# A state-space block: six other first products for GpSimd, and the last state's product with C for VectorE

## The reference, cut to what matters

```
dA = exp(dt_t[:, :, None] * A)
h  = dA * h + (dt_t * x_t)[:, :, None] * B_t[:, None, :]
y  = einsum('bds,bs->bd', h, C_t)
...
y  = y + xc * D_param
y  = y * silu(z)
```

## Time and profile before

| | |
|---|---|
| median of 3 runs | 16611.66 (16605.69 to 16624.14) |
| the profiled execution: time, span | 16605.28, 16603.5 |
| busy: PE, DVE, ACT, POOL | 14390.7 (87%), 15104.1 (91%), 11266.2 (68%), 15002.7 (90%) |
| granted TensorE clock | 0.941 of full |
| DMA | 152 GB/s of HBM traffic over the span |

### The profile page before, as it was taken

The page is one execution under the profiler, slowest core; times in us unless marked ns, Lnnn a source line. Parts: engine busy times, 40 slices in busy tenths (PEclk is TensorE's granted clock), DMA queues, the critical chain, the costliest instruction groups (busy, mean ns, idle before and its releaser), DMA issues. The chain is left out here.

```text
span 16603.5 us, 158027 instructions
## 1 busy us (share of the span) xinstructions
PE 14390.7 (87%) x30720; PEld 5782.7 (35%) x30720; DVE 15104.1 (91%) x13023; ACT 11266.2 (68%) x18635; POOL 15002.7 (90%) x6275
## 2 busy tenths in 40 slices
PE   6888888888888888888888888888888888888888
PEld 2333333333333333333333333333333333333333
DVE  6999999999999999999999999999999999998988
ACT  5666667666666666666677666667666676667675
POOL 5999889998899989998899998999989999899998
PEclk9999999999999999999999999999999999999999
DMA  3444444444444444444444444444444444444443
GB/s 132 155 154 161 150 152 154 155 157 150 154 154 153 163 145 153 156 154 159 142 155 160 152 160 143 156 156 158 155 143 156 156 157 158 146 148 158 150 151 135
DMA packets 738975, 2535.44 MB, mean 153 GB/s; under 512 B 77240, under 2 KB 78016, under 8 KB 721728
## 3 DMA queue, kind: packets, MB, share of 16 engines
q1 hardware_dynamic: 738112, 2527.45, 44.8%
HBM read 2376.15 MB, written 150.99 MB: 152 GB/s over the span
## 5 line engine op out<-in xcount | busy, mean ns | idle before, releaser
L1467 POOL TENSOR_TENSOR RING<-RING,CS 128x1024 f32<-128x1024 f32 x4096 | 9833.9, 2416 | 1369.6 <-DVE RING L1148 1350.2
L1148 DVE TENSOR_TENSOR_SCAN RING<-DA,HS,RING 128x512 f32<-128x512 f32 x8192 | 9955.4, 1264 | 811.0 <-ACT DA L777 614.1
L388 PE MATMUL YP<-RING,EYE 128*128 128x512 f32 x16384 | 8293.4, 638 | 1648.6 <-POOL RING L1467 1578.7
L777 ACT ACTIVATE DA<-ITEM,AN 128x512 f32<-128x512 f32 x8192 | 5519.4, 685 | 3384.9 <-DVE RING L1148 3376.5
L388 PEld LDWEIGHTS YP<-RING,EYE 128*128 128x128 f32 x16384 | 3133.4, 199 | 6324.9 <-issue 3616.5
L1128 DVE TENSOR_TENSOR RING<-DTP,BS 128x1024 f32<-128x1024 f32 x2816 | 3375.5, 1206 | 0.4 <-DMA BS<-bc_rows 0.3
L1454 POOL TENSOR_TENSOR RING<-ITEM,BS 128x1024 f32<-128x1024 f32 x1280 | 3016.6, 2357 | 9.4
L388 PE MATMUL FL<-XN,WC 128*128 128x512 f32 x4096 | 1943.3, 618 | 9.7 <-ACT XN L864 4.6
L388 PEld LDWEIGHTS FL<-XN,WC 128*128 128x128 f32 x4096 | 839.4, 205 | 1129.8 <-issue 1121.5
L791 ACT ACTIVATE ITEM<-FL,COL 128x512 f32<-128x512 f32 x512 | 347.6, 679 | 1183.1 <-PE FL L388 1183.1
L388 PE MATMUL FL<-LS,WP 128*128 128x512 f32 x2048 | 995.6, 610 | 35.3 <-DVE XR L1184 29.2
(11 more groups left out here) (123 smaller groups left out, 10636.4 us busy)
## 6 DMA issues: line engine op xcount, KB each, us to landing
BS<-bc_rows SPq DMA_DIRECT2D x2048, 512.0 KB, 4.9
CS<-bc_rows SPq DMA_DIRECT2D x2048, 512.0 KB, 3.6
XR<-in_x SPq DMA_DIRECT2D x128, 1024.0 KB, 7.3
x_slices<-XR SPq DMA_DIRECT2D x64, 1024.0 KB, 8.1
XR<-x_slices SPq DMA_DIRECT2D x64, 1024.0 KB, 7.5
out<-XR SPq DMA_DIRECT2D x64, 1024.0 KB, 8.2
XR<-in_wqkv SPq DMA_DIRECT2D x24, 1024.0 KB, 7.3
bc_rows<-ROWS SPq DMA_DIRECT2D x256, 64.0 KB, 4.6
```

Of the source, the lines that this page charges most:

```text
L388: return pe.matmul(*a, **k)
L777: act.activation(DA[:, h, :], DT[:, i % 2, h, :], ACT.Exp, scale=AN[:, h, s:s + 1]).then_inc(dA_ready, 1)
L1148: dve.tensor_tensor_scan(H[:, slot(n), h, :], DA[:, h, :], U[:, slot(n), h, :], HS[:, i % ITEMS, h, s:s + 1], ALU.mult, ALU.add).then_inc( ...
L1467: pool.tensor_tensor(G[:, slot(n)], H[:, slot(n)], CS[:, s % C_ROWS, :].unsqueeze(1).broadcast_to([P, NH, T]), ALU.mult).then_inc(g_ready, 1)
```

## The change

VectorE makes the second product of state 15 right behind its own scan 15 (`out_last`), with a semaphore of its own, `g_last`. GpSimd makes only the second products of states 0 to 14. GpSimd's first products are now those of states 1, 3, 5, 7, 8 and 9, six instead of five; VectorE makes ten instead of eleven, and where it makes them is set anew. The waits on `g_ready` are recounted for 15 products a window, and those on the sixteenth go to `g_last`. In SP's queue the second load of C of a window waits for `g_last`, and the first load of B in a window waits for the second product of state 14 of the window before.

```
-POOL_U = (0, 1, 2, 7, 8)
+POOL_U = (1, 3, 5, 7, 8, 9)
-AHEAD = ((), (), (3,), (4, 5), (6,), (), (), (9,), (10,), (11,), (12,), (13,), (14,), (15,), (), ())
-AHEAD_LATE = ((), (), (3,), (4,), (5, 6), (), (), (9,), (10,), (11,), (12,), (13,), (14,), (15,), (), ())
+AHEAD = ((0,), (), (2,), (4,), (6,), (), (), (), (), (10,), (11, 12,), (13,), (14,), (15,), (), ())
+AHEAD_LATE = ((0,), (), (2,), (4,), (), (6,), (), (), (), (10,), (11,), (12, 13,), (14,), (15,), (), ())
...
+        def pool_g(n):
+
+            return n // NS * (NS - 1) + min(n % NS + 1, NS - 1)
...
                 if not (first and q < 2):
-                    sp.wait_ge(g_ready, tile * STEPS + (n - 2))
+                    if q == 1:
+                        sp.wait_ge(g_last, tile * ITEMS + i)
+                    else:
+                        sp.wait_ge(g_ready, tile * (STEPS - ITEMS) + pool_g(n - 3))
...
                     load_c(tile, w, q, first=first)
+                    if q == 0 and not (first and w == 0):
+                        sp.wait_ge(g_ready, tile * (STEPS - ITEMS) + pool_g(w * NS - 2))
...
-                pe.wait_ge(g_ready, tile * STEPS + n + 1)
+                if s == NS - 1:
+                    pe.wait_ge(g_last, tile * ITEMS + i + 1)
+                else:
+                    pe.wait_ge(g_ready, tile * (STEPS - ITEMS) + pool_g(n))
...
                     dve.wait_ge(state_kept, tile * STEPS + (n - used(n) + 1))
-                    dve.wait_ge(g_ready, tile * STEPS + (n - used(n) + 1))
+                    if (n - used(n)) % NS == NS - 1:
+                        dve.wait_ge(g_last, tile * ITEMS + (n - used(n)) // NS + 1)
+                    else:
+                        dve.wait_ge(g_ready, tile * (STEPS - ITEMS) + pool_g(n - used(n)))
...
+            def out_last(tile, i):
+                n = i * NS + NS - 1
+                q = NS // 2 - 1
+                dve.wait_ge(c_landed[q % (C_ROWS // 2)],
+                            tile * rows_count(ITEMS - 1, NS // 2 - 1, C_ROWS // 2) + rows_count(i, q, C_ROWS // 2))
+                dve.wait_ge(g_summed, tile * STEPS + (n - used(n) + 1))
+                dve.wait_ge(scanned, tile * (2 * STEPS) + 2 * (n + 1))
+                dve.tensor_tensor(G[:, slot(n)], H[:, slot(n)],
+                                  CS[:, (NS - 1) % C_ROWS, :].unsqueeze(1).broadcast_to([P, NH, T]),
+                                  ALU.mult).then_inc(g_last, 1)
...
                     scan(tile, n, first=first)
+                    if s == NS - 1:
+                        out_last(tile, w)
...
-                    out_state(tile, n, first=first)
+                    if s < NS - 1:
+                        out_state(tile, n, first=first)
```

More of the change, by code:

```diff
@@ L142, in block_ssm_kernel @@
             sem(n) for n in ("wc_ready", "wp_folded", "dd_ready", "logsmall_ready", "an_exp", "an_ready", "pbf_ps", "pbf_ready", "mean_ready"))
-        u_dve, u_pool, dA_ready, scanned, g_ready, state_kept, g_summed = (
-            sem(n) for n in ("u_dve", "u_pool", "dA_ready", "scanned", "g_ready", "state_kept", "g_summed"))
+        u_dve, u_pool, dA_ready, scanned, g_ready, g_last, state_kept, g_summed = (
+            sem(n) for n in ("u_dve", "u_pool", "dA_ready", "scanned", "g_ready", "g_last", "state_kept", "g_summed"))
         rows_ready, rows_stored, capped = (sem(n) for n in ("rows_ready", "rows_stored", "capped"))
```

## The result

The changed kernel takes 16916.22 us (median, 16906.51 to 16919.33), the kernel before 16616.29 beside it. The ratio is 1.0179, with a 95% interval of 1.0163 to 1.0195: slower by 300 us. The prediction was 16290 and faster; its range ended at 16640. The profiled execution has a span of 16912.4 us, 308.9 more than before.

What follows compares the result with a forecast made beforehand. VectorE and GpSimd, both 92% busy, were taken to bound the kernel by turns. Window changes of +0.1, -2.5, -1.0 and -1.6 us gave -5.0 a tile, -320 over 64 tiles: 16290 us, range 16000 to 16640.

Steps and rivals of the forecast that it cites:

- the flat price of a contention: VectorE's two-SBUF product of state 15 waits for the running GpSimd instruction: 1.2 to 3.5 us, taken as 2.2.
- 2.0 us a window for both hold-ups: On GpSimd, time lost a window to `dt_poly` and G15 together, added to 24 instructions of 2.31 us.
- rival 2: G15 on VectorE starves through several GpSimd instructions: +920 less the 320, 17200 us; chance 0.05.
- a late `dt_x`: Mid-window GpSimd makes `dt_x` late; ScalarE's copy, the exponential of state 14 and scan 14 wait, replacing the gate's wait.
- net 282 us: Extra VectorE work from gaining G15 and losing a first product: 1.1 us a window, 256 times, if waiting stayed unchanged.
- what can be won is waiting only: Across the engines, no engine has less to do after the change, so any gain must come from waits.
- 320 won in spite of 282 of work: Over the kernel, -5.0 us a tile gives -320 in 64 tiles, although VectorE's added work alone would cost 282.
- the gate is set by G14 and TensorE's order: At the window's end, G14, not G15 alone, sets the gate: 8.9 us from start of sum 14 to end of sum 15.
- the gate's and U2's waits go: At the window's head, the gate's wait nearly goes, from 489 us to under 150, and U2 waits for nobody.
- C and B rows are no cause: In SP's queue, C and B loads wait for G15 and G14 but have slack, about 7 us for B; nothing charged.
- j = 1 was forecast at 62.0: Window j = 1, bound by GpSimd, was to take 61.9 to 62 us against 61.9 before, change +0.1.
- Rival 1: GpSimd's stops move to the window's head, G0, G2, G3 each waiting 1.5 us: +250, 16860 us; chance 0.13.

Runs made afterwards that it cites:

- e9: Changed kernel with GpSimd waiting for `dt_poly` ahead of G10, two instructions earlier, everything computed; 16788.63 us, 128 below the changed kernel.
- e1: Changed kernel with `dt_poly` reading DTP (PSUM) and YZ instead of two SBUF sources, polynomial part of dt left out; 16729.85 us.
- e2: Kernel before with `dt_poly` reading DTP (PSUM) and YZ, polynomial part of dt left out; 16261.55 us, ratio 0.9793 to the kernel before.
- e12: e8 with `dt_poly` reading PSUM, polynomial part of dt left out; 15971.45 us, ratio 0.9612.
- e8: Kernel before with U0 and U2 on VectorE, a step ahead, U3 and U5 on GpSimd, G15 staying there; 16454.01 us, ratio 0.9903.
- e7: Changed kernel with U9 back on VectorE and U9 to U12 at the steps of the kernel before; 16723.36 us, 193 below the changed kernel.
- e13: e7 with both `dt_poly` and the product of state 15 reading PSUM, their true contributions left out; 16255.24 us.
- e14: e8 with GpSimd's wait for `dt_poly` ahead of `dt_first`, one instruction earlier than in e11; 16552.97 us, ratio 0.9971.
- e3: Kernel before with only the product of state 15 moved to VectorE, the plan of first products unchanged; 16865.37 us, ratio 1.0155.
- e4: Kernel before with only the new plan of first products, all 16 second products staying on GpSimd; 16894.96 us, ratio 1.0172.
- e6: Changed kernel with U0 made ahead of scan 15 of the window before and U2 ahead of scan 1; 16891.12 us, 25 below the changed kernel.
- e5: e1 with, besides, the product of state 15 reading DTP (PSUM) in place of H, its true contribution left out; 16373.18 us.
- e11: e8 with GpSimd's wait for `dt_poly` ahead of G10, as in e9, everything computed; 16324.17 us, ratio 0.9820.
- e10: Changed kernel with only the product of state 15 reading DTP (PSUM), its contribution left out; 16777.86 us, 138 below the changed kernel.

## Why the prediction was wrong

**The step that failed first** is the flat price of a contention: "So the product waits for the running GpSimd instruction, then holds the next one up", with `dt_poly` left at its old length and 2.0 us a window for both hold-ups. Only the new product was priced; that the old one, `dt_poly`, could change its price was not asked. Its price is 1.2 us beside an idle GpSimd, some 2.4 with a turn at the first boundary, and 4.6 to 7.6 when it is passed over, since then it waits until GpSimd stops. The change moved three first products into GpSimd's steps 0 to 6, so that in j = 1 `dt_poly` is issued while G9 runs, with `dt_first` and G10 behind it: 7.63 us in place of 2.45, +313 us over the kernel. e9 shows that the stop ends it; e1, e2, e9 and e12 show that the length counts. (Most of the +313 us comes with the first step of the table after e12, where U3 and U5 go to the middle: e8 has 236 of them and is faster all the same.) The earlier trace rows had a maximum of 6241 ns for this line, and rival 2 used the mechanism, but for the product of state 15 alone and "Against: line 1165 takes 2.41". In the sum the contention makes about 200 of the 300 us (543 less 345): by the table after e12 132 in the first step and 75 in the third, less 15 in the second.

On the Trainium skill's page "SBUF — State Buffer", section "Who interferes with whom", the second to issue is blocked until the first finishes. The trace differs: 7.63 us is the rest of one GpSimd instruction and two whole ones that began after VectorE's had been issued. By the page the wait would have ended at 4462.0, with G9; the measurement decides.

**The second failure** is that the wait for the exponential was expected at scan 14, behind a late `dt_x`. It rose by 222 us in all, but at scan 14 it fell from 117 to 80 us, and ScalarE's wait for `dt_x` fell from 244 to 174: `dt_x` was not late. The exponentials are late at steps 4, 5 and 8. Of these e7 and e13 show that step 8 goes with the move of U9 to U12, 193 and 118 us. The rise at steps 4 and 5 is there in e8 too (318 us; 182 before), so it comes with the move of U0, U2, U3 and U5, which e8 shares; what it costs was not tried. The working had followed each engine's count of instructions, but not which of VectorE's products stood beside ScalarE's front work. That a late `dt_x` does cost time is seen only in e14.

**The third failure is the product of state 15.** It was taken at 2.2 us and took 1.72, so its net 282 us were 132; with `dt_poly` gone it takes 3.02 (e1), with the old plan 2.07 (e3). But it was to be paid for by the waits that it ends, and it is not. e3 shows that without the new plan it leaves the gate where it was, e4 that with the new plan the kernel takes as long without it (1.0172 and 1.0179), and e7 beside e8 that it costs 269 us although the gate's wait falls by 165 (240 to 74). Without contention it costs 284. The prediction had said that "what can be won is waiting only". Its own terms, 320 won in spite of 282 of work, need some 600 us less of waiting on VectorE; VectorE's idle time fell by 163 us (1499 to 1337).

**What held:** the gate is set by G14 and TensorE's order (e3, e4); the gate's and U2's waits go, 534 us; C and B rows are no cause (11 us of GpSimd's waits are for C).

**The windows.** j = 1 was forecast at 62.0, j = 2 at 64.9, j = 3 at 62.3, j = 0 at 58.5; in the tile shown they take 65.0, 67.9, 65.4 and 61.1. In the mean over all tiles j = 0 changed by -1.2 (-1.6 was forecast), j = 1 by +2.0 (+0.1), j = 2 by +1.4 (-2.5) and j = 3 by +2.7 (-1.0), so only j = 0 came as forecast. In j = 3 the prediction allowed 0.7 us of waits on VectorE; in the tile shown it idles 5.65 (65.40 less 59.75).

**Rival 1** gave nearly the time (16860), and its sign came true: GpSimd idles as long as before (1341 us for scans, 1350 before). Its mechanism is there in part. The waits of GpSimd's second products at steps 0 to 3 rose from 302 to 613 us, those of G0 alone from 60 to 421, while those at steps 9 and 10 fell from 575 to 274. But in its sum GpSimd's hold-ups are the whole loss, 256 us; measured, GpSimd is busy 150 us more (15153; 15003 before) and idle 159 more. That its time is so close is luck in part. The own-product wait of 0.3 us was not in the sum at all; e6 shows that to remove it gives 25 us.

**What stays open.** What decides whether the waiting instruction has its turn at the first boundary is not settled. In j = 2 of the changed kernel it was passed over 1.2 us after it was issued, in the earlier trace rows it had its turn after 1.3. The 111 us by which e5 is behind e2 are no single cause: by the table after e12 they are -290, +284 and +118. The 118 are shown to go with U9 to U12 together; which of the four moves them, and what of it is GpSimd's product less, was not tried.

## What to carry to other kernels

An instruction that contends has no price of its own: ask what the other engine has ready behind the boundary at which it arrives, for every such instruction in the kernel and not only for the new one. Where two engines are equally full, as here, look whether work that is moved to close a wait has been covering a third engine's work. An exchange that leaves the counts equal is not free: the product of state 15 cost VectorE's full work, and the time that it freed on GpSimd turned into idle time. Before an instruction is moved off a late engine, look whether it is the one that the waiting engine needs, or stands behind it: here G14 set the gate, and freeing G14 alone won 158 us (e8; 292 with the earlier stop, e11) where moving G15 lost.

## What the runs showed of the hardware

VectorE's instruction with two SBUF sources can be passed over by up to two further GpSimd instructions that were issued after it, 7.63 us for 1.2 us of work, and its end follows GpSimd's next stop by 1.1 us (the changed kernel and e9). With one source in PSUM the same shape took 1.18 to 1.23 us every time, with GpSimd busy 87 to 92% of the span (`dt_poly` in e1, e2, e5, e12 and e13, the first products in all kernels, the product of state 15 in e5, e10 and e13). Making `dt_poly` read PSUM is worth 345 us in the kernel before (e2) and 483 in e8 (e12), and both times GpSimd's second products get shorter as well (mean 2416 ns before and 2362 in e2, 2404 in e8 and 2372 in e12).
